# DLRM interaction and top tower: raw w1 and w2 exchange buffers, and tables 3 and 4 are split earlier

## What is computed

```python
e = jnp.stack([tbl_0[ids[:, 0]], ..., tbl_25[ids[:, 25]]], axis=1)      # 2048 x 26 x 128
combined = jnp.concatenate([dense_output[:, None, :], embeddings], axis=1)
interactions = jnp.einsum('bfd,bgd->bfg', combined, combined)
interactions_flat = interactions[:, iu, ju]                             # 351 pairs, upper triangle
z = jnp.concatenate([dense_output, interactions_flat], axis=1)
h = jnp.concatenate([z, r_dense_output], axis=1)                        # 607 columns
h = jnp.maximum(h @ W_top1 + b_top1, 0.0)                               # 512
h = jnp.maximum(h @ W_top2 + b_top2, 0.0)                               # 256
y = h @ W_top3                                                          # 1
```

## Time and profile before

| | |
|---|---|
| median of 3 runs | 379.1 us (377.99 to 379.31) |
| the profiled execution | 381.57 us, its span 379.7 us |
| mean granted TensorE clock | 0.995 |
| PE busy | 340.2 us (90%) |
| DVE / ACT / POOL busy | 243.6 (64%) / 147.4 (39%) / 248.6 us (65%) |
| the chain that ended last | PE 83%, DMA 6%, DVE 4%, issue 3% |

### The profile page before, as it was taken

The page is one execution under the profiler, slowest core; times in us unless marked ns, Lnnn a source line. Parts: engine busy times, 40 slices in busy tenths (PEclk is TensorE's granted clock), DMA queues, the critical chain, the costliest instruction groups (busy, mean ns, idle before and its releaser), DMA issues.

```text
span 379.7 us, 15229 instructions
## 1 busy us (share of the span) xinstructions
PE 340.2 (90%) x6472; PEld 325.0 (86%) x6472; DVE 243.6 (64%) x308; ACT 147.4 (39%) x305; POOL 248.6 (65%) x265
## 2 busy tenths in 40 slices
PE   0078676999999999999999999999999999999996
PEld 0077565999889997999989998999989998999996
DVE  3559766797547926597357936597357926696133
ACT  2246543543334314533335224533334315523431
POOL 6737778777777777777777776677767776770000
PEclk9999998999999999999999999999999999999999
DMA  7985729543232424233233432333232332110000
GB/s 167 244 196 158 173 71 288 160 111 103 57 96 78 111 77 92 76 89 96 64 98 79 104 87 67 82 94 87 71 86 76 111 80 60 49 48 7 0 2 1
DMA packets 20607, 36.05 MB, mean 95 GB/s; under 512 B 7698, under 2 KB 9490, under 8 KB 20596
## 3 DMA queue, kind: packets, MB, share of 16 engines
q1 hardware_dynamic: 12260, 18.84, 18.3%
q0 software_dynamic: 8192, 16.79, 17.5%
q10 hardware_dynamic: 144, 0.26, 0.6%
HBM read 35.87 MB, written 0.01 MB: 94 GB/s over the span
## 4 chain that ended last, share of the span: by engine, by line
PE 83%; DMA 6%; DVE 4%; issue 3%; SPq 1%; ACT 1%; POOL 1%; DVEq 0%; POOLq 0%
PE oh_ps L672 39%; PE work_ps L698 14%; PE work_ps L745 11%; PE tr_ps L683 6%; PE work_ps L787 5%; PE work_ps L710 3%; DMA emb_t<-table 3%; DVE onehot L526 2%; DVE lo L539 1%; PE work_ps L727 1%; DMA gram<-w 1%; DMA pairs<-table 1%; SPq L240 1%; POOL emb L315 1%; DMA emb<-table,ids_sb 1%
## 5 line engine op out<-in xcount | busy, mean ns | idle before, releaser
L315 POOL DMA_INDIRECT emb<-table,ids_sb x256 | 247.7, 968 | 92.1 <-issue 77.8
L526 DVE TENSOR_TENSOR onehot<-ids_b,rows_ps 125x1024 fp32r<-125x1024 int32 (+1 forms) x160 | 189.9, 1240 | 35.2 <-PE oh_ps L672 29.6
L672 PE MATMUL oh_ps<-onehot,hi 125*128 125x256 f32 x656 | 166.2, 292 | 28.9 <-issue 21.2
L672 PE MATMUL oh_ps<-onehot,lo 125*128 125x256 f32 x656 | 161.1, 284 | 0.0
L672 PEld LDWEIGHTS oh_ps<-onehot,hi 125*128 125x128 f32 x656 | 126.0, 192 | 32.6 <-issue 22.6
L672 PEld LDWEIGHTS oh_ps<-onehot,lo 125*128 125x128 f32 x656 | 126.4, 193 | 0.0
L377 ACT ACTIVATE emb_t<-oh_ps 128x256 f32<-128x256 f32 x80 | 51.2, 643 | 107.7 <-PE oh_ps L672 106.0
L698 PE MATMUL work_ps<-emb_t 128*32 128x26 f32 x4096 | 55.8, 196 | 7.5 <-ACT gram L398 3.5
L698 PEld LDWEIGHTS work_ps<-emb_t 128*32 128x32 f32 x4096 | 47.2, 110 | 16.4 <-issue 9.1
L566 DVE SCALAR_TENSOR_TENSOR top_in<-work_ps,top_in 128x512 fp32r<-128x512 f32 x14 | 9.6, 688 | 56.1 <-ACT top_in L420 56.1
L393 ACT ACTIVATE emb_t<-tr_ps 128x512 f32<-128x512 f32 x64 | 43.3, 748 | 0.0
(11 more groups left out here) (108 smaller groups left out, 237.7 us busy)
## 6 DMA issues: line engine op xcount, KB each, us to landing
ids_b<-ids_t SPq DMA_DIRECT2D x39, 256.0 KB
emb<-table,ids_sb POOLq DMA_INDIRECT x256, 2.5
emb_t<-table SPq DMA_DIRECT2D x3, 448.0 KB
dense_sb<-dense_t SPq DMA_DIRECT2D x8, 128.0 KB
emb<-table SPq DMA_DIRECT2D x2, 448.0 KB
gram<-table SPq DMA_DIRECT2D x2, 448.0 KB
pairs<-table SPq DMA_DIRECT2D x2, 448.0 KB
gram<-w SPq DMA_DIRECT2D x1, 768.0 KB
```

The lines of the kernel that those rows point to most:

```text
L315: pool.indirect_dma_start(emb[:, i, s, :], None, tables[t], bass.IndirectOffsetOnAxis(ap=ids_sb[:, i, t:t + 1], axis=0),).then_inc(gathere ...
L526: dve.tensor_tensor(onehot[:, n % ONEHOT_BUFFERS, 0:h, :], ids_b[0:CHUNK_ROWS, u, :].unsqueeze(1).to_broadcast([CHUNK_ROWS, h, PAIR]), row ...
L672: mm = pe.matmul(oh_ps[u % 2][:, 0, :], part[:, CHUNK_BASE[u] + chunk, :], onehot[:, (HALVES * u + s) % ONEHOT_BUFFERS, c, :], start=chunk ...
```

## The change

Raw w1 now lies in `pairs` (which grows from 1280 to 1536 columns for it), raw w2 in `gram`. SP issues w2 as soon as the last low part of a table is made, ahead of the wait for tile 1's gathers; the other weights follow behind that wait. ACT splits w2 before the first copies of the Gram, takes two Gram quarters, splits w1, takes the other two; DVE makes w2's low part first, and w1's low part, the constant columns and the low part of `w1_dense` after the one-hots for step 1. ACT's wait for the constant columns moves from ahead of its loop to the first `take_turn`. In the start, ACT makes the high parts of tables 0 to 4 in one row, and DVE the low parts of 3 and 4 before the one-hots of table 2.

```diff
--- before.py
+++ after.py
@@ -116,7 +116,7 @@
         ident = sb("ident", [P, P])
         zero = sb("zero", [P, 1])
         gram = sb("gram", [P, SIDE, 2, QUADS])
-        pairs_home = sb("pairs", [P, max(SHARE * COLUMNS, max(CHUNKS) * D)])
+        pairs_home = sb("pairs", [P, max(SHARE * COLUMNS, max(CHUNKS) * D, 3 * H1)])
         pairs = pairs_home[:, 0:SHARE * COLUMNS].rearrange("l (j c) -> l j c", j=SHARE)
 
         top_in = sb("top_in", [P, 4, 2, PAIR], f32r)
@@ -139,8 +139,8 @@
         pairs_row = pairs_home[:, :]
         w1_dense = h2[:, :, :].rearrange("p a n -> p (a n)")
 
-        w1_raw = gram_row[:, 0:3 * H1].rearrange("p (k n) -> p k n", k=3)
-        w2_raw = pairs_row[:, 0:N1 * H2].rearrange("p (k n) -> p k n", k=N1)
+        w1_raw = pairs_row[:, 0:3 * H1].rearrange("p (k n) -> p k n", k=3)
+        w2_raw = gram_row[:, 0:N1 * H2].rearrange("p (k n) -> p k n", k=N1)
 
 
         whole = CHUNKS[0] * D
@@ -263,14 +263,14 @@
             load_dense(0)
             sp.wait_ge(onehot_ready, 2 * HALVES)
             spread_ids(1, 0)
+            sp.wait_ge(lo_made, ONE)
+            sp.dma_start(w2_raw, w2.rearrange("(k p) n -> p k n", p=P)).then_inc(w2_ready, 16)
 
             for g in range(NG):
                 sp.wait_ge(gathered[1][g], 16 * GROUP)
-            sp.wait_ge(lo_made, ONE)
             sp.dma_start(w1_raw, w1[D:D + 3 * P, :].rearrange("(k p) n -> p k n", p=P)).then_inc(w1_ready, 16)
             sp.dma_start(w1_dense, w1[0:D, :]).then_inc(w1_dense_ready, 16)
             sp.dma_start(w1_twice[:, :], w1[D + 3 * P:D + 3 * P + D, :]).then_inc(w1_dense_ready, 16)
-            sp.dma_start(w2_raw, w2.rearrange("(k p) n -> p k n", p=P)).then_inc(w2_ready, 16)
             sp.dma_start(b2_sb[:, :], b2.rearrange("(a n) -> a n", a=1).to_broadcast([P, H2])).then_inc(vectors_ready, 16)
             sp.dma_start(w3_sb[:, :], w3.rearrange("(a n) o -> a (n o)", a=1).to_broadcast([P, H2]))\
               .then_inc(vectors_ready, 16)
@@ -420,11 +420,10 @@
                 act.activation(h1_parts(f)[0], work_ps[H1_BANK[f]].rearrange("p (a n) -> p a n", a=2), ACT.Relu)\
                    .then_inc(h1_hi_made, 1)
 
-            for u in range(IN_EMB_T + 1):
+            for u in range(OWN_HOMES):
                 table_hi(u)
             act.wait_ge(lo_made, IN_EMB_T)
             take_onehot(0, 0)
-            table_hi(4)
             take_slots(0, 0, 0)
             take_slots(0, 0, 1)
             take_onehot(0, 1)
@@ -452,23 +451,24 @@
             take_onehot(0, 9)
             take_slots(0, 1, 2)
             take_slots(0, 1, 3)
+            act.wait_ge(w2_ready, 16)
+            act.activation(w2_sb[0][:, :, :], w2_raw, ACT.Copy).then_inc(w_hi_made, 1)
+
+            act.wait_ge(w_lo_made, 1)
+            for u in range(2):
+                take_gram(0, 0, u)
             act.wait_ge(w1_ready, 16)
             act.activation(w1_sb[0][:, 0:3, :], w1_raw, ACT.Copy).then_inc(w_hi_made, 1)
-
-            act.wait_ge(w_lo_made, 1)
-            for i in range(2):
-                for u in range(2):
-                    take_gram(0, i, u)
+            for u in range(2):
+                take_gram(0, 1, u)
             act.wait_ge(w1_summed, 1)
             act.activation(w1_sb[0][:, 3, :], w1_dense, ACT.Copy).then_inc(w_hi_made, 1)
-            act.wait_ge(w2_ready, 16)
-            act.activation(w2_sb[0][:, :, :], w2_raw, ACT.Copy).then_inc(w_hi_made, 1)
-            act.wait_ge(columns_made, 2)
 
             with act.Fori(1, STEPS) as b:
                 take_onehot(b, 0)
                 take_slots(b, 0, 0)
                 take_slots(b, 0, 1)
+                act.wait_ge(columns_made, 2)
                 take_turn(b - 1, 0)
                 take_onehot(b, 1)
                 put_dense(b)
@@ -589,15 +589,15 @@
             table_lo(0)
             table_lo(1)
             table_lo(2)
-            first_onehot(2)
             table_lo(3)
             table_lo(4)
+            first_onehot(2)
             for u in range(3, ONE):
                 first_onehot(u)
                 if u + 2 < ONE:
                     table_lo(u + 2)
             dve.wait_ge(w_hi_made, 1)
-            dve.tensor_tensor(w1_sb[1][:, 0:3, :], w1_raw, w1_sb[0][:, 0:3, :].bitcast(f32), ALU.subtract)\
+            dve.tensor_tensor(w2_sb[1][:, :, :], w2_raw, w2_sb[0][:, :, :].bitcast(f32), ALU.subtract)\
                .then_inc(w_lo_made, 1)
             make_table(1, 0)
             make_table(1, 1)
@@ -605,16 +605,16 @@
             dve.wait_ge(w1_dense_ready, 2 * 16)
             dve.tensor_tensor(w1_dense, w1_dense, w1_twice[:, :], ALU.add).then_inc(w1_summed, 1)
             dve.wait_ge(w_hi_made, 2)
+            dve.tensor_tensor(w1_sb[1][:, 0:3, :], w1_raw, w1_sb[0][:, 0:3, :].bitcast(f32), ALU.subtract)\
+               .then_inc(w_lo_made, 1)
+            dve.wait_ge(w_lo_made, 2)
+            dve.memset(pairs[:, :, FILLED:FILLED + 1], 1.0).then_inc(columns_made, 1)
+            dve.memset(pairs[:, :, FILLED + 1:COLUMNS], 0.0).then_inc(columns_made, 1)
+            dve.wait_ge(columns_made, 2)
+            dve.wait_ge(w_hi_made, 3)
             dve.wait_ge(w1_summed, 1)
             dve.tensor_tensor(w1_sb[1][:, 3, :], w1_dense, w1_sb[0][:, 3, :].bitcast(f32), ALU.subtract)\
                .then_inc(w_lo_made, 1)
-            dve.wait_ge(w_hi_made, 3)
-            dve.tensor_tensor(w2_sb[1][:, :, :], w2_raw, w2_sb[0][:, :, :].bitcast(f32), ALU.subtract)\
-               .then_inc(w_lo_made, 1)
-            dve.wait_ge(w_lo_made, 3)
-            dve.memset(pairs[:, :, FILLED:FILLED + 1], 1.0).then_inc(columns_made, 1)
-            dve.memset(pairs[:, :, FILLED + 1:COLUMNS], 0.0).then_inc(columns_made, 1)
-            dve.wait_ge(columns_made, 2)
             dve.wait_ge(vectors_ready, 2 * 16)
             dve.sem_inc(y_made, 1)
```

## The result

| | before | after |
|---|---|---|
| median of six runs | 379.08 us (377.99 to 379.46) | 376.91 us (375.69 to 377.42) |
| ratio | | 0.993, 95% interval 0.9908 to 0.9952 |
| profiled execution, span | 381.57, 379.7 us | 376.75, 374.9 us |

By the medians the changed kernel is 2.2 us faster, by the interval 1.8 to 3.5 us. The spans of the two profiles differ by 4.8 us, more than twice that; the second profile of before further down shows why one must not explain all of it.

The account below looks back on a forecast made before the run. PE's own list of work was taken to bound the kernel from the step of b = 1 on, DVE's list ahead of it from 24.89. 2.75 + 0.34 - 0.3 - 0.6 = 2.2 us off 379.1 gave 376.9 us, range 375.2 to 379.2.

Parts of the forecast that it names:

- the weights' part: Between the Gram's halves: PE's stall all but gone, 2.75 us, and 0.34 for the clock; 3.7 without the table term.
- the table term: In the start: ACT and DVE stand for table 4, landing at 24.4; everything behind on DVE 0.6 us later (-1.3 to +1.6).
- The bound: From the step of b = 1 on PE's own work sets the pace; only the time of entering this can move.
- the 0.34 us for the clock: Gram's second half, behind the stall: two quarters at the lower clock take 4.15 us against 3.81; this 0.34 is gained.
- Rival A: In the start: table 4 lands at 21.7, the table term is +1.3, nothing lost on gathers: 374.1 us, chance 0.13.
- The gathers at step 1's transposes: PE wants step 1's last gather at 66.5, it lands at 65.5 to 68.1: 0.3 us of stall (0 to 1.6).
- POOL's lag in the fifth turn: Fifth turn's Gram: POOL gains less than PE, so most of the 1.0 us from its idle stretch is lost: 0.6.
- The low parts did hold it longer: Low parts from table 5 on may block POOL's gathers: its 1.65 us shrinks to 0.6, time 377.6 us instead of 376.8.

Follow-up runs that it names:

- e2: The kernel before with only the early high and low parts of tables 3 and 4: 377.14 us, ratio 0.994.
- e3: The changed kernel again, no edit, for a second profile of it: 376.70 us, ratio 0.9929.
- e4: The kernel before again, no edit, a single execution for a second profile of it: 379.36 us, span 377.5.
- e5 to e12: Eight runs of four edits to the changed kernel, on three other chips where every kernel took about 500 to 520 us; ratios to before 0.9884 to 1.0049.

## Why the prediction was right, and where it was not

The time came out as forecast (376.9 against 376.91 us), and that is luck: the weights' part was put too large, a cost for POOL was taken off that did not come, and the table term had the wrong sign, and these made up for each other. The prediction named its own test for the whole: it fails if the tables' order turns out to gain. The order did gain, 2.6 us in e2. Of its other signs of being right, those on the weights came: PE's idle ahead of the Gram's second half is gone, no lower clock stands there, and w1's DMA is out of the chain. Those on the tables and on POOL did not: high part 4 started at 21.88 (22.35 in e3) and not at 24 to 25, where 22 or before was a sign of being wrong, and no Gram turn near 7.3 us was lost. Step 1's first unit started at 62.66 (63.32 in e3), forecast near 64.0.

**The bound, and the place of the gain: right.** From the second Gram on, all six profiles need 279.1 to 279.7 us. All of the change lies ahead of it.

**The weights' part: mechanism right, size too large.** The stall between the Gram's halves is gone, no lower clock stands in the Gram, w1's split lies beside Gram quarters, and w2 was there in time. The distance from the first Gram to step 1's transposes fell by 2.85 us against the first profile of before and by 1.98 against the second, where the sum had 3.46 + 0.34 less 0.1 = 3.7. The stall in the row, 3.46 us, belonged to one execution; in the other it was 2.16. And the Gram in one piece takes 8.60 us where I had put two halves of 3.81, the shortest half of all: the halves of e2, both at the full clock, take 4.21 and 4.12. With that the 0.34 us for the clock has no support either: the second half of before, in part at the lower clock, took 4.15, about as long as e2's at the full one.

**The table term: wrong in sign.** This is the step that failed, and in it the landing of table 4, put at 24.4, that is 5.5 us behind high part 3. Measured: high part 4 starts 4.23, 4.32 and 3.92 us behind high part 3. Low part 4 follows it by 1.1 us, the one-hots of tables 2 and 3 run in one piece, low part 5 starts 10.9 to 11.2 us behind high part 3 instead of 11.5 to 11.7, and low part 9 comes 0.6 to 1.5 us earlier instead of 0.6 later. The bounds that I gave (21.7 to 25.4) held; inside them the byte count was misread. I took the 0.97 MB that the queue moved between tables 1 and 2 as what the pair of broadcast and table needs. The pair is 256 and 500 KB, 0.77 MB, so the rest belonged to other transfers; at the 0.19 MB per microsecond of the earlier trace rows 0.77 MB take 4.1 us (an estimate made afterwards). Between the starts of high parts 3 and 4 the queue moved 0.90 MB in the changed kernel and 0.75 in e2 (17.65 to 21.88 and 18.06 to 21.98 us), not 0.99. In what order the queue moves its transfers no run shows. Rival A had the sign. Its landing, 2.8 us behind high part 3, was about as far off as mine, but its term, +1.3, lies inside the 0.6 to 1.5 us that low part 9 moved.

**Why A's 374.1 did not come.** A added its table term to the whole of the weights' term, which was itself too large. The parts also overlap. The times only hint at it: 1.0 us alone and 2.6 us alone make 3.0 together (medians; ratios 0.9976, 0.994, 0.9929), and the missing 0.6 us lies within the intervals. The profiles show it. The table part starts POOL 2.6 to 2.9 us earlier against high part 3; tile 1's gathers land earlier, w1's DMA goes out earlier, and the stall that the exchange was to remove is already down to 0.69 us. The other way round, the exchange without earlier gathers runs PE into the gathers of step 1. That one removes the other's price was in none of my cases.

**The gathers at step 1's transposes: right.** 0.3 us was forecast. The changed kernel's eight transposes take 1.37 us (1.15 in e3) where they took 1.04, in the first profile with a landing of 8.32 us ahead of them, longer than the 4.0 to 6.1 of the earlier trace rows.

**POOL's lag in the fifth turn: wrong.** I took 0.6 us off for it, and nothing was lost: the Gram of the fifth turn takes 7.25 us in the changed kernel and 7.22 in e3, before 7.30 and 7.39. Against high part 3, POOL had gained 2.6 to 2.9 us at tile 1's first gather, not 1.4. The low parts did hold it longer afterwards, as the prediction feared, but by less: from the first to the last start of tile 1's sixteen gathers it needed 21.7 and 22.3 us, before 21.4 and 21.3. Where it stood for the Gram one turn earlier, in the first profile, that brought nothing either: that Gram took 8.30 us, before 8.29. The last column is as before.

**The lower clock in units 8 and 9: not foreseen.** Ahead of unit 8 PE stands 2.0 to 2.7 us. In the first profile of before (2.7) the granted clock stayed at 1.00 behind that, as in e2 (2.0); in four of six profiles it fell to the lower level (1.2 GHz) there. From low part 9 to the Gram these four need 9.48 to 9.71 us, the other two 8.86 and 8.88: 0.6 to 0.85 us, in the kernel before as in the changed one. The Trainium skill, TensorE: Matmul & The Clock Gate, section "Part 1: The HAM clock gate", says of the slow matmuls at the start of a kernel that their number differs from run to run of the same kernel. Here it is another place of the kernel, but the two profiles of before differ in the same way: one has the lower clock in units 8 and 9, the other not.

So the account is: forecast -0.6 + 3.7 - 0.3 - 0.6 = 2.2. Measured on one chip (e4 to e3, up to the second Gram): +0.64 from the list, -0.06 for the clock, +1.98 at the Gram, +0.55 behind it, and -0.65 because high part 3 came later in that execution: 2.46 us, of which the last is not the change's. Without it the sum is 3.1 us, near the 3.0 between the medians on that chip. What the 0.55 behind the transposes comes from is open.

## What to carry to other kernels

When two edits aim at one wait, price each with the other in place: here 2.6 and 1.0 us alone made 3.0, and on top of the table part the exchange brought 0.4 us, which the runs can't tell from nothing. Take no stall and no landing from a single profile if the sum is a matter of one or two microseconds; a second profile of the same kernel moved both by over a microsecond. Before an instruction is moved up, ask what its data wait for, and bound the landing from both sides; if the sign hangs on it, that is the first thing to measure. When a landing is read from the bytes that a queue has moved, set beside them the bytes of the transfers in question: the difference belongs to others. A total that comes out right says nothing of its terms.

## What the runs showed of the hardware

- A gather (indirect DMA on POOL) that starts while DVE runs an instruction with two operands in SBUF ends about 0.8 us behind that instruction. Before: the gather of 2.50 us in the earlier trace rows behind w1's low part. In the changed kernel: low part 9 takes the time from 44.42 to 45.91, and the gather at 45.26 takes 1.47 us instead of 0.94. In the six profiles of the table above every gather of over 1.1 us overlaps such an instruction. Beside one-hots, whose second operand is in PSUM, gathers keep their 0.94 us, and so does one that starts before the low part does (in before at 30.43, the low part at 30.57).

```profile
45.26 1.47 POOL L315 DMA_INDIRECT emb<-table,ids_sb  x1 [0.30 <-issue]
```

- The Gram's 512 small matmuls take 8.1 to 8.6 us beside running gathers, 7.1 to 7.4 where POOL stands for 1.6 to 2.2 us of them, and 5.06 us in the last turn of before, where POOL has nothing left to do (timeline of PE):

```profile
356.79 5.06 PE L698 MATMUL work_ps<-emb_t 128*32 128x26 f32 x512
```

  What in the gathers slows them was not tried.
- On three chips (e5 to e12) the same program took a third longer, with PE waiting for issue. Its cause is unknown; a study of single microseconds can't be made there.
